# The order of fill, scores and outputs in the fourth step of a head pair

## What is computed

```python
x = layernorm(x + (adj @ x) @ weight + bias)                   # layer 0
q, k, v = split(x @ w_qkv)                                     # 8 heads of 64
attn = softmax(where(adj == 0, -inf, q @ k.T * 64 ** -0.5))    # per head, 512 x 512
o = (attn @ v) @ w_proj + b_proj
x = layernorm(x + o + layernorm(o) * ln_gamma + ln_beta)       # layer 1
```

## Time and profile before

| | us |
|---|---|
| median of 3 runs | 3365.83 |
| lowest, highest | 3362.24, 3365.88 |
| the profiled execution | 3366.38 |
| its span, first to last instruction | 3364.6 |

### The profile page before, as it was taken

The page is one execution under the profiler, slowest core; times in us unless marked ns, Lnnn a source line. Parts: engine busy times, 40 slices in busy tenths (PEclk is TensorE's granted clock), DMA queues, the critical chain, the costliest instruction groups (busy, mean ns, idle before and its releaser), DMA issues. The chain is left out here.

```text
span 3364.6 us, 88016 instructions
## 1 busy us (share of the span) xinstructions
PE 3308.5 (98%) x31792; PEld 2923.1 (87%) x31792; DVE 2623.7 (78%) x6434; ACT 2229.6 (66%) x4634; POOL 1997.1 (59%) x2690
## 2 busy tenths in 40 slices
PE   8999999998999999999999999999999999999996
PEld 6888888886899998889899899899999899998894
DVE  7666666665788888888888888888888888888887
ACT  4444444444677777777777777777777777777775
POOL 4555556552466666666666666666666666666666
PEclk8999999998999999999999999999999999999998
DMA  5565555653011111111122211111111111111210
GB/s 188 174 195 168 186 187 172 190 180 102 27 52 51 55 54 51 51 55 51 51 63 66 66 51 51 51 51 51 51 54 54 51 51 54 51 51 53 70 59 32
DMA packets 345217, 279.62 MB, mean 83 GB/s; under 512 B 13713, under 2 KB 275857, under 8 KB 344977
## 3 DMA queue, kind: packets, MB, share of 16 engines
q1 hardware_dynamic: 344976, 275.83, 27.0%
HBM read 141.56 MB, written 134.22 MB: 82 GB/s over the span
## 5 line engine op out<-in xcount | busy, mean ns | idle before, releaser
L1126 ACT ACTIVATE pt_hi<-bank 128x512 fp32r<-128x512 f32 x1024 | 557.0, 596 | 546.3 <-PE bank L835 533.9
L1119 ACT ACTIVATE probs<-probs,bias_row 128x512 f32<-128x512 f32 x1024 | 731.7, 721 | 44.7 <-DVE bias_row L1239 43.6
L1259 DVE TENSOR_TENSOR pt_lo<-bank,pt_hi 128x512 fp32r<-128x512 f32 x1024 | 658.0, 684 | 44.0 <-PE bank L858 34.3
L721 POOL TENSOR_SCALAR probs<-probs,inv_sums 128x480 f32<-128x480 f32 (+1 forms) x1024 | 685.3, 682 | 0.0
L1239 DVE CUSTOM_DVE_ANT_0 probs<-bank,mask_bias 128x512 f32<-128x512 f32 x1024 | 661.9, 684 | 9.7 <-PE bank L819 5.8
L718 POOL TENSOR_TENSOR probs<-probs,inv_sums 128x32 f32<-128x32 f32 x512 | 122.7, 240 | 730.4 <-DVE inv_sums L1248 730.3
L872 PE MATMUL bank<-x_lo,w_hi 64*128 64x512 f32 x1024 | 403.3, 394 | 0.0
L870 PE MATMUL bank<-x_lo,w_hi 64*128 64x512 f32 x1024 | 403.3, 394 | 0.0
L872 PE MATMUL bank<-x_hi,w_hi 64*128 64x512 f32 x992 | 403.2, 406 | 0.0
L870 PE MATMUL bank<-x_hi,w_hi 64*128 64x512 f32 x992 | 401.6, 405 | 0.0
L835 PEld LDWEIGHTS bank<-ident,probs 64*128 64x128 f32 x8192 | 362.9, 139 | 40.8 <-issue 4.9
(11 more groups left out here) (139 smaller groups left out, 10847.2 us busy)
## 6 DMA issues: line engine op xcount, KB each, us to landing
x_in<-in_x_dram SPq DMA_DIRECT2D x32, 1024.0 KB, 5.2
u_beta_rows<-ub SPq DMA_DIRECT2D x32, 1024.0 KB, 4.4
ut_hi<-ut_hi_sb SPq DMA_DIRECT2D x128, 256.0 KB, 4.1
ut_lo<-ut_lo_sb SPq DMA_DIRECT2D x128, 256.0 KB, 3.8
x_lo<-ut_lo SPq DMA_DIRECT2D x128, 256.0 KB, 4.7
out_dram<-o SPq DMA_DIRECT2D x128, 256.0 KB, 3.2
ub_row<-u_beta_rows SPq DMA_DIRECT2D x124, 256.0 KB, 2.7
x_hi<-ut_hi SPq DMA_DIRECT2D x124, 256.0 KB, 4.4
```

The costliest lines, as they stand in the source:

```text
L721: pool.tensor_scalar(probs[:, k % 2, a, cols], probs[:, k % 2, a, cols], inv_sums[:, k % 4, a:a + 1], 0.0, ALU.mult, ALU.add)\
L1119: act.activation(probs[:, k % 2, a, :], probs[:, k % 2, a, :], ACT.Exp, bias=bias_row[:, k % 4, a:a + 1], scale=-1.0, accum_out=sums[:, k ...
L1126: act.activation(turned_into(pt_hi, k, i), turned(i), ACT.Copy).then_inc(pthi_made, 1)
L1259: dve.tensor_tensor(turned_into(pt_lo, k, i), turned(i), f32(turned_into(pt_hi, k, i)), ALU.subtract).then_inc(ptlo_made, 1)
```

## The change

In `last_step` (the fourth) eight pairs of the next group's fill are issued in a row, in front of both output runs, where it was six in front and two between the runs; the scores are issued between the two runs and not behind them. In `first_step` the fill behind the scores has six pairs (12 to 17) and not four, and in `second_step` there are nine before and nine behind the scores (18 to 35), and not ten and ten.

```diff
@@ first_step
                         scores_ahead(k)
-                        fill_and_wait(group, 12, 4, k + 1)
+                        fill_and_wait(group, 12, 6, k + 1)
@@ second_step
                         if filled(group):
-                            fill(group, 16, 10)
+                            fill(group, 18, 9)
                         scores_ahead(k)
-                        fill_and_wait(group, 26, 10, k + 1)
+                        fill_and_wait(group, 27, 9, k + 1)
@@ last_step
                         if more_fill:
-                            fill(group + 1, 0, 6)
+                            fill(group + 1, 0, 8)
...
                         attend_v(b, group, pt_hi, 0)
-                        if more_fill:
-                            fill(group + 1, 6, 2)
+
+                        scores_ahead(k, turn_next=True)
                         attend_v(b, group, pt_hi, 1)
-                        scores_ahead(k, turn_next=True)
```

## The result

The changed kernel takes 3381.26 us (median; 3379.51 to 3381.83), the kernel before 3365.44 in the same comparison: ratio 1.0048, 95% interval 1.0035 to 1.0061, that is +15.8 us. The forecast was 3378.0 (+12), with a range of 3368 to 3385.

A forecast was written before the change was run, and what follows sets the result against it. The prediction took PE, busy for 98% of the span, as the bound, so only waits count. Its terms 27.4 - 3.1 - 12.1 - 0.5 gave +11.7, taken as +12 us: 3378.0 us, range 3368 to 3385.

The forecast's parts named there:

- The bound: Whole kernel: PE is busy for 98% of the span, so the change acts through waits on PE alone.
- The held score pair: Fourth steps of groups 0, 2, 3: the third score pair waits for DVE's pt_lo; 93 x 0.294 = +27.4 us.
- Group 1 and the first output run: Group 1's fourth step: no hold, first output run stops waiting for pt_hi; 30 x 0.10 = -3.1 us.
- The first steps: First steps: two more fill pairs ahead of the pt_lo wait remove its stall; about 0.40 a batch, -12.1 us.
- two fill pairs fewer in the second step: zero: Second step: its own wait keeps most of its more than a microsecond of room, so zero cost.
- The ends: Program ends: batch 0 group 0 +0.4, last batch and batch 0's group 1 about -0.9 together; -0.5.
- 1 (the lead absorbs the wait): Fourth-step wait: PE's queued instructions cover it, so the array only gains; -25 us, 3341; chance 0.06.
- 2: Fourth step: DVE's pt_lo ends 0.1 to 0.2 us earlier, so near nothing changes; about 3366; chance 0.09.
- 4: Fourth-step stall costs more where another wait is just met: 0.1 more in 93 steps, +21, 3387; chance 0.06.
- 3: PE clock: stalls of 0.3 us three times a batch let it fall; +155, 3521; chance 0.02.

The follow-up runs named there:

- experiment 2: Kernel before with only the fourth step changed (eight fill pairs in front, scores between the output runs): 3388.74 us, ratio 1.0072.
- experiment 3: Changed kernel with the wait for pt_lo and the probabilities moved behind the second output run, scores left between the runs: 3338.26 us, ratio 0.9925.
- experiment 5: Changed kernel with the fourth step's wait one score pair earlier, before the second pair instead of the third: 3405.36 us, ratio 1.0121.
- experiment 1: Kernel before with only the fill sizes of first and second step changed (6, then 9 and 9 pairs), old fourth step: 3358.17 us, ratio 0.998.
- experiment 6: Kernel of experiment 3 with eleven fill pairs ahead of the second step's scores and seven behind, instead of nine and nine: 3337.13 us.
- experiment 8: Kernel of experiment 3 with five fill pairs behind the first step's scores, then ten and nine in the second step: 3337.26 us.
- experiment 7: Kernel of experiment 3 with seven fill pairs ahead of the second step's scores and eleven behind: 3388.45 us, ratio 1.0068.
- experiment 4: Changed kernel, PE order untouched, with DVE's pt_lo ahead of its two maxima in the fourth step: 3440.43 us, ratio 1.0226.

## Why the prediction was right

**The bound** was right: PE, and on it mostly waits. Its busy time is the same to the tenth in both pages; that it is so to the tenth is in part chance, since held steps have a slow pair more and first steps one less.

**The held score pair** was right in mechanism, place and size: +0.29 a step forecast, +0.305 to +0.318 measured. The small excess is mostly DVE's, whose pt_lo ends 3.96 to 3.97 after the step's start and not the 3.93 to 3.94 of the earlier trace rows; the third pair stands 0.147 behind that and the run 0.307 behind the pair, in every one of these batches. Experiments 2, 3 and 5 show the cause from three sides: alone, taken away, and made larger.

**Group 1 and the first output run**: -0.127 against -0.10. The output runs there took 0.91 (mean), where I had carried over the 0.93 of the second run in the earlier trace rows; four pairs of such a run don't always take the same time.

**The first steps** were right: the stalls are gone. A first step takes 5.346 to 5.363; against its length before with two more pairs of 0.227 that is 0.09, 0.03, 0.16 and 0.13 less in groups 0 to 3, together the 0.40 of the forecast. The PE timeline at the end of group 2's first step, the answer to the earlier trace rows, shows even spacing:

```profile
2041.64 0.39 PE L870 MATMUL bank<-x_hi,w_hi 64*128 64x512 f32 x1
...
2041.86 0.39 PE L870 MATMUL bank<-x_lo,w_hi 64*128 64x512 f32 x1
...
2042.09 0.39 PE L870 MATMUL bank<-x_hi,w_lo 64*128 64x512 f32 x1
...
2042.32 0.68 PE L835 MATMUL bank<-ident,probs 64*128 64x64 f32 x15
```

**The term that was mis-sized is "two fill pairs fewer in the second step: zero".** It cost 0.02 to 0.06 in each of four second steps, 0.15 a batch, 4 us, which is about the distance from +12 to +16. The small differences of the other terms (held pair +1.5 us, group 1 -0.8, third steps -1.3) nearly cancel, which is luck. In the second steps of the changed kernel the pairs from the scores on are 0.227 to 0.238 apart, where the kernel before has 0.226 to 0.229 there. What sets this isn't shown: experiments 1, 3 and 6 have 0.02 to 0.03 of it with nine and with eleven pairs ahead, and only experiment 8, with ten, has none. The third steps, 0.047 shorter in a batch where zero was forecast, stay unexplained too. In experiment 1 the second steps lost 0.06 a batch, the third and fourth 0.10, and the half that was forecast at -12.1 us brought -6.5.

Two slips in the working change nothing: 93 x 0.294 is 27.3 and not 27.4, and the 0.91 us for four pairs at full pace isn't in the earlier trace rows; it is four times 0.227.

**The ends** were forecast at -0.5 and are small: batch 0 is 0.9 longer, the last batch 1.3 shorter. No experiment bears on them.

The rivals: 1 (the lead absorbs the wait) is refuted by the rows of the changed kernel, though its time, 3341, is near the one that experiment 3 reached by moving the wait (3338). 2 and 4 didn't come about: pt_lo's end is 0.01 to 0.03 later and not 0.1 to 0.2 earlier, and a held step costs 0.31 and not 0.4. 3: the granted clock over 2000 to 3000 us of the changed kernel is 1.00, as in the earlier trace rows, with three holds a batch:

```profile
2000.00:3000.00 1000.00, 994.34 (x10827) 937.24 (x10825) 820.33 (x2102) 737.43 (x1600) 611.66 (x896) 1.00 0.19 55
```

The earlier trace rows show the stretch behind the clock's fall and not the one ahead of it: in the kernel before, PE was busy for 1.22 us of the 4 us from 3300 to 3304, at a granted clock of 1.00, and from 3304 to 3308 the clock was 0.52. The holds of the changed kernel leave PE busy for 994 of 1000 us.

The Trainium skill, TensorE: Matmul & The Clock Gate, section "Architectural detail", calls PE's queue a partial reorder window that can pull weight loads ahead of matmuls in flight. The traces agree in that no matmul from behind a held wait ran early, and they show that its weight loads didn't either. The weights of the third score pair in the fourth step of group 0, first in the changed kernel, where its matmuls start at 2016.15, then in experiment 3, where they start at 1991.63:

```profile
2016.12 0.21 PEld L819 LDWEIGHTS bank<-k_hi,q_lo 64*128 64x128 f32 x2 [0.54 <-issue]
```

```profile
1991.41 0.20 PEld L819 LDWEIGHTS bank<-k_hi,q_lo 64*128 64x128 f32 x2
```

Held, the weights are loaded 0.03 ahead of the matmuls; not held, 0.22 ahead. The queue's depth of 64 can't be read from the traces.

## What to carry over

When instructions move on an engine that never idles, list the waits that move with them, and for each the time between what it waits for and its new place: a wait that cost nothing with 0.88 us of room costs 0.45 when a 0.92 us run is put behind it, and the step lost 0.31 after what the rest of the reorder gave. A wait belongs directly ahead of what needs it; here the reorder and the wait could be parted by an edit of three lines, and the same reorder went from +16 to -26 us. When a wait is moved forward, the weight loads behind it are held as well, so even a wait that clears just in time costs a slow pair (group 1 in experiment 5). And look at every wait of a moved block, its first instruction's too: the scores had one on the maxima, which decided two of the experiments.

## What the runs showed of the hardware

A held matmul pair starts 0.15 us after the end of DVE's row (0.135 after its semaphore) in the fourth steps of the changed kernel and of experiments 2 and 5 and in the second steps of experiment 7, and the next pair 0.31 us later instead of 0.23, whether the hold was nothing, 0.06 us or 0.6 us long. The first score pair of experiment 4 differs: it starts 0.05 after the maxima's last row (0.04 after the semaphore), with its successor 0.34 later. All the pairs that started 0.15 behind wait for two semaphores, as `ptlo_made` and `probs_made`, and this one for `max_found` alone. That the second semaphore makes the difference fits these traces; no run tested it.

Pairs of 64x512 matmuls don't keep one pace at a granted clock of 1.00. In the first 2 us or so of fill after the transposes, and after a hold, they are 0.224 to 0.236 us apart, mostly over 0.23; later they settle at 0.227, in most first, second and third steps by 2.4 to 3 us after the transposes' start, but in second steps with nine pairs ahead of the scores only after 4 us or more. I had taken 0.23 for one number; over four second steps in 28 batches the difference between the two kernels is worth some 4 us.
